# Attention stage of a sandwich layer: a loop over two halves written out, with the second half's taps interleaved with the first half's last products

## The chip, the cores and the metric

One core of one Trainium2 chip runs the whole program in one launch. The metric is device time in microseconds. Engines: PE is the matrix engine (with its weight loads, PEld, beside it), DVE the vector engine, ACT the scalar engine, POOL the GpSimd, and SP issues most transfers. Each engine runs its own instructions in program order; they meet at semaphores.

## What is computed

x is 4 x 2048 rows of 256 floats. The first layer makes, for each row and head, 31 softmaxed weights from the row itself and sums the 31 rows up to it with them; the second is a mixture of experts behind a router. Everything is float32.

```python
def _L0_attn_ref(x, w_lin):                       # H = 16 heads, K = 31 taps, P = 30, R = 16
    w = jnp.einsum('btc,fc->btf', x, w_lin).reshape(B, T, H, K)
    w = jax.nn.softmax(w.astype(jnp.float32), axis=-1).astype(x.dtype)
    ...
    kidx = s_idx - t_idx + P
    mask = (kidx >= 0) & (kidx < K)
    ...
    out = jnp.einsum('bhts,bhsr->bhtr', we, xh)
...
def _L0_ffn_ref(...):                             # 16 experts, top 2, and a shared expert
    shared = jax.nn.silu(x @ shared_w_gate.T) * (x @ shared_w_up.T) @ shared_w_down.T
    shared = shared * jax.nn.sigmoid(x @ shared_gate_w.T)
    logits = x @ gate_w.T
    ...
    out = expert_out + shared
x = x + _layernorm(_L0_attn_ref(_layernorm(x), w_lin))
x = x + _layernorm(_L0_ffn_ref(_layernorm(x), ...))
```

## The kernel before

The program has six parts in a row, each closed by a block: `attention`, `routing`, shared experts with the scatter, experts, and the shared-and-combine part. Only `attention` is touched. It computes both the first layer and, row by row, the normalised input `yn` of the second layer, its turned copy `ynt` and the router's logits.

`attention` works in two halves of 4096 rows (`HALVES`), in a hardware loop `Fori(0, HALVES)` on every engine. Each half has two stages.

**Taps stage**, 16 steps (`NPR`), each of two tiles of 128 rows (`u`). SP loads x (`load_x`), DVE takes mean and variance (`moments`), POOL makes scale and shift (`scales1`: add, subtract, power, multiply), ACT normalises (`normal`) into `xn`, SP stores it to a scratch tensor (`store_xn`). PE transposes it (`turn_x`), ACT and DVE split the result in a high and a low part (`high`, `low`), PE multiplies each tile with the weights in three products per half of the channels (`taps`: 12 matmuls of 512 columns a step), DVE takes the maximum and subtracts it (`spread`), ACT takes the exponential (`exps`), PE transposes it (`turn_e`, 8 transposes) and ACT copies it to `probs` (`keep`). The weights `wraw` are loaded once, split by ACT into `wh` (line 415) and by DVE into `wl` (line 328).

**Products stage**, 16 steps (`NCH`), each of two tiles (`t`). SP loads x's normalised rows back in four transfers (`load_xs`, into `xbd`) and the residual x (`load_xr`). DVE spreads the probabilities over a band with a mask (`masked`, four operations), PE multiplies (`products`, 128 matmuls of 68 columns in two groups of 64, line 528), DVE divides by the sums and takes moments (`divided`), POOL makes scales (`scales23`), ACT normalises (`centred`), POOL adds the residual (`residual`), DVE takes the moments of the sum (`moments3`), ACT makes `yn` (`normal2`), PE transposes it (`turn_yn`, line 541), ACT copies it to `ynt` (`turned`, line 474), PE multiplies it with the router weights (`router`, line 548), ACT copies the result to `logits` (`put_logits`, line 453), SP stores x2, yn and ynt. This chain is spread over seven steps by the offsets given to `skewed`: with offset -5, `turn_yn` in step i works on tile pair i - 5. Within a step each engine's order is the order of the arguments. `skewed` writes the first and last steps of a stage out and puts the middle ones in a loop, four steps to a turn.

```python
skewed(pe, NCH, (-5, turn_yn), (0, lambda i, q: products(i, q, 0)), (-5, router),
       (0, lambda i, q: products(i, q, 1)))
skewed(act, NCH, (-6, put_logits), (-2, centred), (-4, normal2), (-5, turned))
skewed(ve, NCH, (1, masked), (-1, divided), (-2, moments3))
skewed(po, NCH, (-2, residual), (-1, scales23), (-3, nothing))
```

PSUM has eight banks `pb`. In the taps stage the transposed x has banks 0 and 1, the logits of the taps 2 to 5, the transposed exponentials 6 and 7; in the products stage the products have 0 to 3, and `psy` (the turned yn of tile t and beside it its router result) banks 6 and 7. Since each stage drains before the next begins, the banks can be given twice.

Ahead of the loop POOL sets all constants (among them zeros in `xbd`, line 262, and the masks, lines 273 to 281); SP and PE wait for all of them (`CONSTS`), and PE also for the whole of `wl` and for the router weights. ACT issues eight small transfers (line 418) that give the store semaphores their first value. Behind the loop DVE runs the search for the two best experts on the first 56 of 64 tiles (`top.find`, lines 118 to 124).

## Time and profile before

| | |
|---|---|
| median of three runs | 1187.29 us (1184.39 to 1193.31) |
| profiled execution | 1188.04 us, of which the profile's span is 1186.0 |
| busy over the span | PE 982.8 us (83%), DVE 808.8 (68%), ACT 581.0 (49%), POOL 482.3 (41%) |
| granted PE clock, mean | 0.92 |
| attention part | 0 to 436.7 us of the span |
| bytes moved | 188.07 MB, mean 159 GB/s |

How to read it: the busy shares are means over stages with different limits, so each stretch is read by itself. Times are from the span's start. An idle time in square brackets stands before the operation and names who ended it.

### The profile page before, as it was taken

What the parts mean: (1) busy time and instruction counts of PE and PEld (TensorE: products, weight loads), DVE (VectorE), ACT (ScalarE), POOL (GpSimd) and SP (SyncE); (2) the same over time, 40 slices, a digit from 0 to 9 for tenths busy, and PEclk for the clock granted to TensorE, in tenths of its full rate; (3) what the DMA queues carried; (4) which work ended last, traced back from release to release, by engine and by line L of the source; (5) the groups of instructions that cost most, each with busy time, mean ns of one, the idle gap of its engine ahead of it and who ended that gap; (6) DMA issues with size and microseconds to landing.
All of it is one profiled execution on the core that took longest, in us unless ns stands there. A gap on an engine that the chain in (4) does not pass through costs nothing. (4 is left out here: it accounts for less than half of the span.)

```text
span 1186.0 us, 31172 instructions
## 1 busy us (share of the span) xinstructions
PE 982.8 (83%) x9192; PEld 849.6 (72%) x9193; DVE 808.8 (68%) x2070; ACT 581.0 (49%) x1308; POOL 482.3 (41%) x725
## 2 busy tenths in 40 slices
PE   3998798499879840799999869998999799989981
PEld 2777686377678830688888768888888687878771
DVE  3887987188798779444445347777777468777765
ACT  3993344499534441344444435554555345444442
POOL 5221445222054533576676500000000357888774
PEclk9998999599999955899999989999999899989995
DMA  3333577443247762757565454555555435656553
GB/s 107 108 99 81 152 209 213 131 120 108 64 129 219 213 216 98 232 188 242 191 201 173 153 142 155 160 161 160 153 162 160 151 116 178 183 188 183 174 162 106
DMA packets 189971, 188.07 MB, mean 159 GB/s; under 512 B 56256, under 2 KB 171072, under 8 KB 189632
## 3 DMA queue, kind: packets, MB, share of 16 engines
q1 hardware_dynamic: 173232, 150.30, 42.2%
q0 software_dynamic: 12288, 33.57, 8.6%
q10 hardware_dynamic: 4368, 3.16, 0.9%
q8 instruction: 43, 0.70, 0.3%
q14 instruction: 40, 0.33, 0.1%
HBM read 100.81 MB, written 86.15 MB: 158 GB/s over the span
## 5 line engine op out<-in xcount | busy, mean ns | idle before, releaser
L903 POOL DMA_INDIRECT sorted_rows<-yr,sl x128 | 133.6, 1044 | 81.5 <-issue 38.0
L1192 POOL DMA_INDIRECT cy<-expert_rows,csl x128 | 138.8, 1085 | 45.4 <-issue 44.2
L528 PE MATMUL bank<-xbd,am 128*32 128x68 f32 x4096 | 138.5, 304 | 11.3 <-DVE am L367 4.4
L528 PEld LDWEIGHTS bank<-xbd,am 128*32 128x32 f32 x4096 | 122.8, 129 | 18.6 <-DVE am L367 10.9
L1185 POOL MEMSET czero<- 128x4 f32 x1 | 0.1, 102 | 257.8 <-POOLq L968 257.8
L1065 PE MATMUL bank<-eh,xh 128*128 x288 | 95.3, 331 | 0.7 <-DVE xl L1109 0.7
L367 DVE TENSOR_TENSOR am<-probs,mask 128x512 f32<-128x512 f32 x128 | 82.5, 707 | 18.8 <-PE bank L528 9.3
L805 DVE TENSOR_TENSOR s_hf<-s_sg,bank 128x512 f32<-128x512 f32 (+1 forms) x48 | 33.0, 688 | 88.3 <-ACT s_sg L780 88.3
L287 POOL TENSOR_TENSOR rstd<-mv,eps 128x2 f32<-128x2 f32 (+1 forms) x68 | 13.5, 198 | 187.3 <-DVE mv L359 110.9
L1109 DVE TENSOR_TENSOR xl<-bank,xh 128x256 fp32r<-128x256 f32 x144 | 61.2, 425 | 41.7 <-ACT xh L1091 40.7
L1091 ACT ACTIVATE xh<-bank 128x256 fp32r<-128x256 f32 x144 | 55.5, 385 | 67.8 <-PE bank L1038 67.6
L458 ACT ACTIVATE av<-av,shift,rstd 128x256 f32<-128x256 f32 x64 | 35.0, 595 | 105.6 <-POOL shift L292 105.6
L1038 PE MATMUL bank<-ident,xg 128*128 128x128 f32 x288 | 56.8, 280 | 33.6 <-issue 22.6
L1065 PE MATMUL bank<-el,xh 128*128 x288 | 82.3, 286 | 0.0
L1065 PE MATMUL bank<-eh,xl 128*128 x288 | 82.0, 285 | 0.0
L823 PE MATMUL bank<-c_yh,gh 128*128 128x512 f32 x176 | 73.4, 417 | 6.3 <-DVE c_yl L797 6.3
L302 POOL TENSOR_TENSOR x<-av,xr 128x256 f32<-128x256 f32 x64 | 47.4, 761 | 72.4 <-ACT yn L466 69.5
L823 PE MATMUL bank<-s_yh,gh 128*128 128x512 f32 x176 | 71.0, 403 | 6.1 <-DVE s_yl L797 6.1
L782 ACT ACTIVATE c_hh<-c_hf 128x512 fp32r<-128x512 f32 (+1 forms) x48 | 30.3, 632 | 91.3 <-DVE c_hf L805 91.3
L834 PE MATMUL bank<-dh,c_hh 128*128 128x256 f32 (+1 forms) x192 | 58.6, 305 | 19.0 <-DVE c_hl L810 19.0
L823 PE MATMUL bank<-c_yl,gh 128*128 128x512 f32 x176 | 72.0, 409 | 0.0
L823 PE MATMUL bank<-c_yh,gl 128*128 128x512 f32 x176 | 71.5, 406 | 0.0
(198 smaller groups left out, 3155.8 us busy)
## 6 DMA issues: line engine op xcount, KB each, us to landing
xg<-sorted_rows SPq DMA_DIRECT2D x144, 128.0 KB, 2.1
expert_rows<-yo SPq DMA_DIRECT2D x144, 128.0 KB, 1.8
xbd<-xn_scratch SPq DMA_DIRECT2D x128, 72.0 KB, 2.2
xt<-x SPq DMA_DIRECT2D x32, 256.0 KB, 2.7
xn_scratch<-xn SPq DMA_DIRECT2D x64, 128.0 KB, 2.5
xr<-x SPq DMA_DIRECT2D x32, 256.0 KB, 3.2
x_scratch<-x SPq DMA_DIRECT2D x32, 256.0 KB, 3.2
yn_scratch<-yn SPq DMA_DIRECT2D x32, 256.0 KB, 3.1
```

Source lines behind the costliest of these rows:

```text
L302: nc.gpsimd.tensor_tensor(x2[:, q, t], av[:, q, t], xr[:, q, t], ALU.add).then_inc(s["x2_ok"], 1)
L367: nc.vector.tensor_tensor(am[:, q, g], probs[:, bass.ds(i * CB, CB), g, None, :].to_broadcast([P, CB, 2, J]), mask[:, None].to_broadcast([ ...
L458: nc.scalar.activation(av[:, q, t], av[:, q, t], ACT.Identity, scale=rstd2[:, q, t:t + 1], bias=shift2[:, q, t:t + 1]).then_inc(s["z_ok"], 1)
L528: ins = nc.tensor.matmul(pso[q][t][J * b:J * b + J, g * MW:(g + 1) * MW], am[:, q, g, e, side], xbd[:, q, e + side, :, g], start=(g == 0 a ...
L823: ins = self.nc.tensor.matmul(self.pb[2 * k + half][:], w[:, c, col:col + P], y[:, q, c, :], start=(j == 0), stop=(j == 5))
L834: ins = self.nc.tensor.matmul(o, a[0:f, g, t * P:(t + 1) * P], w[0:f, m, :], start=(m == 0 and t % 2 == 0 and j == 0), stop=(m == FT - 1 a ...
L903: nc.gpsimd.indirect_dma_start(out=xg_d, out_offset=bass.IndirectOffsetOnAxis(ap=sl[:, q, t, u, k:k + 1], axis=0), in_=yr[:, t, u], in_off ...
L1038: ins = nc.tensor.transpose(px[r % 2][:, c * P:(c + 1) * P], xg[:, r, c * P:(c + 1) * P], ident[:])
L1065: ins = nc.tensor.matmul(pg[r % 2][:, 0:2 * MF], a[:, r % 2, c * P:(c + 1) * P], w[:, bass.ds(e, 1), c * C:(c + 1) * C], start=(j == 0), s ...
L1091: nc.scalar.activation(xh[:, r % 2], px[r % 2][:, 0:C], ACT.Copy).then_inc(s["xh_ok"], 1)
L1109: nc.vector.tensor_tensor(xl[:, r % 2], px[r % 2][:, 0:C], xh[:, r % 2].bitcast(F32), ALU.subtract).then_inc(s["xl_ok"], 1)
L1192: nc.gpsimd.indirect_dma_start(out=y[:, v, k, j], out_offset=None, in_=yg_d, in_offset=bass.IndirectOffsetOnAxis(ap=sl[:, v, k, j:j + 1], ...
```

## The change

The loop over halves and the loops inside it are gone; each engine's instructions are written out in one common order, `flow`. It goes through the taps steps of half 0, its product steps, and from product step 13 on sets a taps step of half 1 (beginning with -4, whose only work is a load of x) behind each product step, up to product step 22, which is past the last work of half 0. The remaining taps steps and the product steps of half 1 follow. To let both stages be in flight, the banks are shared out anew: both transposed tiles of x share bank 0, the transposed exponentials have banks 1 and 6, both `psy` tiles share bank 7, and tiles of one bank are waited for as a pair. The router's offset goes from -5 to -6, and it now stands at the head of PE's step, `turn_yn` between the two groups of products. The router's result overwrites the turned rows.

At the start the weights are loaded in two parts on ACT's queue, split in two parts, and PE waits for each where it first uses it; x's first load waits for no constants; POOL sets xbd, the masks and other constants in the first taps steps (`places`). The eight first stores are gone, and the padding rows of all four sequences are stored once.

```diff
-        psx, psl, pse = pb[0:2], (pb[2:4], pb[4:6]), pb[6:8]
-        pso, psy = (pb[0:2], pb[2:4]), pb[6:8]
+        psx, psl, pse = (pb[0][:, 0:C], pb[0][:, C:2 * C]), (pb[2:4], pb[4:6]), (pb[1], pb[6])
+        pso, psy = (pb[0:2], pb[2:4]), (pb[7][:, 0:C], pb[7][:, C:2 * C])
...
+        def flow(taps_step, product_step):
+            for i in range(-4, NPR):
+                taps_step(0, i)
+            for j in range(2):
+                taps_step(0, NPR + j)
+                product_step(0, j - 2)
+            for i in range(NCH - 3):
+                product_step(0, i)
+            for i in range(NCH - 3, NCH + 7):
+                product_step(0, i)
+                taps_step(1, i - NCH - 1)
+            for i in range(6, NPR):
+                taps_step(1, i)
+            for j in range(2):
+                taps_step(1, NPR + j)
+                product_step(1, j - 2)
+            for i in range(NCH + 7):
+                product_step(1, i)
+
+        def at(h, i, f):
+            if 0 <= i < 16:
+                f(h * 16 + i)
...
-            sp.dma_start(wraw[:], wd).then_inc(s["w_in"], 16)
-            sp.dma_start(gws[:], gw).then_inc(s["gw_in"], 16)
-            sp.wait_ge(s["consts"], CONSTS)
...
+            def load_xs(n):
+                q = n % 2
+                if n == 0:
+                    wait_apart(sp, s["sp_passed"], s["padded"], 64)
+                    wait_apart(sp, s["sp_passed"], s["places_ok"], PLACES)
+                if n % NCH == 0:
+                    for k in range(2):
+                        wait_apart(sp, s["sp_passed"], s[f"xn_out{k}"], (n // NCH + 1) * (NPR * 16))
+                sp.wait_ge(s["pso_full"], n + 1)
...
+            def taps_step(h, i):
+                at(h, i + 4, load_x)
+                at(h, i + 2, store_xn)
+                if h == 0 and i == 0:
+                    sp.dma_start(gws[:], gw).then_inc(s["gw_in"], 16)
+                    sp.wait_ge(s["zeros"], 1)
+                    for a in range(BATCH):
+                        sp.dma_start(xn_d[a, 0], zero[0:J, 0:C]).then_inc(s["padded"], 16)
+
+            def product_step(h, i):
+                at(h, i + 2, load_xs)
+                at(h, i, load_xr)
+                at(h, i - 2, store_x2)
+                at(h, i - 4, store_yn)
+                at(h, i - 5, store_ynt)
+            flow(taps_step, product_step)
...
-            nc.gpsimd.memset(xbd[:], 0.0).then_inc(s["consts"], 1)
...
+            def places(i):
+                if i == 0:
+                    nc.gpsimd.memset(xbd[:, 0], 0.0).then_inc(s["places_ok"], 1)
+                if i == 1:
+                    nc.gpsimd.memset(xbd[:, 1], 0.0).then_inc(s["places_ok"], 1)
+                if i == 2:
+                    nc.gpsimd.memset(ones[:], 1.0).then_inc(s["consts"], 1)
+                    nc.gpsimd.memset(mask[:], 1.0).then_inc(s["consts"], 1)
+                    nc.gpsimd.iota(top.iota[:], pattern=[[-1, E]], base=E, channel_multiplier=0).then_inc(s["consts"], 1)
+                    po.wait_ge(s["consts"], 6)
+                    po.wait_ge(s["places_ok"], 2)
+                if 3 <= i < 3 + HS:
+                    k = i - 3
+                    part = slice(32 * k, 32 * k + 32)
+                    po.wait_ge(s["norm_ok"], i + 4)
+                    nc.gpsimd.memset(xbd[part, :, :, SLOT_C + k:SLOT_C + k + 1, :], 1.0).then_inc(s["places_ok"], 1)
...
+            def low(n):
+                ve.wait_ge(s["xth_ok"], n * 2 + 2)
+                for u in range(2):
+                    nc.vector.tensor_tensor(xtl[:, n % 2, u], psx[u], xth[:, n % 2, u].bitcast(F32),
+                                            ALU.subtract).then_inc(s["xtl_ok"], 1)
...
+            def taps_step(h, i):
+                at(h, i - 1, spread)
+                at(h, i + 1, low)
+                at(h, i + 3, moments)
+                if h == 0 and i == -2:
+                    for c in range(CC):
+                        ve.wait_ge(s["w_hi"], c + 1)
+                        nc.vector.tensor_tensor(wl[:, c], wraw[:, c], wh[:, c].bitcast(F32), ALU.subtract).then_inc(s["w_lo"], 1)
+
+            def product_step(h, i):
+                at(h, i + 1, masked)
+                at(h, i - 1, divided)
+                at(h, i - 2, moments3)
+            flow(taps_step, product_step)
...
+            for c in range(CC):
+                act.dma_start(wraw[:, c], wd[:, c]).then_inc(s[f"w_in{c}"], 16)
...
-            nc.scalar.activation(wh[:], wraw[:], ACT.Copy).then_inc(s["w_hi"], 1)
-            act.wait_ge(s["zeros"], 1)
-            for k, name in enumerate("xn_out0 xn_out1 x2_out0 x2_out1 yn_out0 yn_out1 ynt_out0 ynt_out1".split()):
-                act.dma_start(first_d[k], zero[:, 0:4]).then_inc(s[name], 16)
...
+            def high(n):
+                for u in range(2):
+                    m = n * 2 + u
+                    act.wait_ge(s["psx_full"], n * 2 + 2)
+                    act.wait_ge(s["psl_full"], m + 1)
+                    nc.scalar.activation(xth[:, n % 2, u], psx[u], ACT.Copy).then_inc(s["xth_ok"], 1)
...
+            def put_logits(n):
+                for t in range(2):
+                    m = n * 2 + t
+                    act.wait_ge(s["psg_full"], n * 2 + 2)
+                    nc.scalar.activation(logits[:, m:m + 1, :], psy[t][:, None, 0:GW], ACT.Copy).then_inc(s["lg_ok"], 1)
...
+            def taps_step(h, i):
+                at(h, i - 2, keep)
+                at(h, i + 1, high)
+                at(h, i - 1, exps)
+                if h == 0 and i == -2:
+                    weights_high(0)
+                at(h, i + 2, normal)
+                if h == 0 and i == -2:
+                    weights_high(1)
+
+            def product_step(h, i):
+                at(h, i - 6, put_logits)
+                at(h, i - 2, centred)
+                at(h, i - 4, normal2)
+                at(h, i - 5, turned)
+            flow(taps_step, product_step)
...
-            pe.wait_ge(s["consts"], CONSTS)
-            pe.wait_ge(s["w_lo"], 1)
-            pe.wait_ge(s["gw_in"], 16)
...
-                skewed(pe, NPR, (-2, turn_e), (1, turn_x), (0, taps))
...
-                skewed(pe, NCH, (-5, turn_yn), (0, lambda i, q: products(i, q, 0)), (-5, router),
-                       (0, lambda i, q: products(i, q, 1)))
...
+            def turn_x(n):
+                if n == NPR:
+                    pe.wait_ge(s["av_ok"], (NCH - 1) * 2 + 4)
+                for u in range(2):
+                    m = n * 2 + u
+                    pe.wait_ge(s["xn_ok"], m + 5)
+                    pe.wait_ge(s["xtl_ok"], n * 2 + 2)
...
+            def turn_yn(n):
+                for t in range(2):
+                    m = n * 2 + t
+                    pe.wait_ge(s["yn_ok"], m + 5)
+                    pe.wait_ge(s["lg_ok"], n * 2 + 2)
...
+            def router(n):
+                if n == 0:
+                    pe.wait_ge(s["gw_in"], 16)
+                pe.wait_ge(s["ynt_ok"], n * 2 + 2)
+                for t in range(2):
+                    for c in range(CC):
+                        ins = nc.tensor.matmul(psy[t][:, 0:GW], ynt[:, n % 2, t, c], gws[:, c, :],
+                                               start=(c == 0), stop=(c == CC - 1))
+                    ins.then_inc(s["psg_full"], 1)
...
+            def taps_step(h, i):
+                at(h, i - 2, turn_e)
+                at(h, i + 1, turn_x)
+                at(h, i, taps)
+
+            def product_step(h, i):
+                at(h, i - 6, router)
+                at(h, i, lambda n: products(n, 0))
+                at(h, i - 5, turn_yn)
+                at(h, i, lambda n: products(n, 1))
+            flow(taps_step, product_step)
```

## Rows read from the trace of the kernel before

**Rows 1.** Busy time by windows: start:end, length, each engine's busy us, granted clock, DMA share, GB/s

```profile
137.02:202.36 65.34, 58.95 (x1405) 51.83 (x1402) 54.62 (x156) 30.04 (x81) 31.29 (x60) 1.00 0.70 204
202.36:235.98 33.62, 16.16 (x68) 12.01 (x69) 7.33 (x27) 14.63 (x39) 9.15 (x24) 0.54 0.45 147
...
350.84:416.05 65.21, 60.15 (x1405) 53.04 (x1402) 54.08 (x156) 31.28 (x83) 31.33 (x61) 0.97 0.72 210
416.05:436.70 20.65, 13.30 (x60) 10.38 (x60) 15.40 (x27) 9.81 (x30) 7.35 (x16) 0.60 0.50 170
22.20:95.20 73.00, 72.31 (x366) 55.77 (x365) 62.38 (x148) 68.47 (x116) 17.23 (x56) 1.00 0.39 108
```

**Rows 2.** Waits from 140 to 200 us: total us, times, longest

```profile
PE bank L548 <- ACT ynt L474: 6.4, 6, 1.7
...
ACT yn L466 <- DMA yn_scratch<-yn: 2.2, 2, 1.1
```

**Rows 3.** Timeline of product steps: start us, us, engine, line, operation, count, idle time before

```profile
101.21 8.53 PE L528 MATMUL bank<-xbd,am 128*32 128x68 f32 x256 [2.19 <-DVE am L367]
...
126.57 0.92 PE L541 MATMUL bank<-ident,yn 128*128 128x128 f32 x4 [1.03 <-ACT yn L466]
...
162.79 0.66 PE L541 MATMUL bank<-ident,yn 128*128 128x128 f32 x4
...
163.06 2.50 DVE L367 TENSOR_TENSOR am<-probs,mask 128x512 f32<-128x512 f32 x4 [0.73 <-PE bank L528]
...
163.38 2.19 PE L528 MATMUL bank<-xbd,am 128*32 128x68 f32 x64
164.17 1.08 ACT L466 ACTIVATE yn<-x,shift,rstd 128x256 f32<-128x256 f32 x2
165.16 0.63 ACT L474 ACTIVATE ynt<-bank 128x256 f32<-128x256 f32 x2
...
165.50 1.41 POOL L302 TENSOR_TENSOR x<-av,xr 128x256 f32<-128x256 f32 x2 [2.37 <-ACT yn L466]
...
165.58 1.07 PE L548 MATMUL bank<-gws,ynt 128*128 128x18 f32 x8
...
166.33 0.19 ACT L453 ACTIVATE logits<-bank 128x18 f32 x1 [0.54 <-PE bank L548]
...
167.91 0.75 DVE L399 BATCH_NORM_STATS2 st<-x 128x6 f32<-128x256 f32 x2
```

**Rows 4.** Timeline of the start

```profile
0.81 1.28 ACT L411 ACT_TABLE_LOAD   x1 [0.81 <-PEq L1352]
...
5.68 1.91 ACT L415 ACTIVATE wh<-wraw 128x2048 fp32r<-128x2048 f32 x1 [3.59 <-DMA wraw<-wd]
5.69 3.75 ACTq L418 DMA_DIRECT2D first_stores<-zero  x8
...
7.63 2.35 DVE L328 TENSOR_TENSOR wl<-wraw,wh 128x2048 fp32r<-128x2048 f32 x1 [7.63 <-ACT wh L415]
...
12.24 7.47 SPq L207 DMA_DIRECT2D xt<-x  x3
15.06 0.75 DVE L356 BATCH_NORM_STATS2 st<-xt 128x6 f32<-128x256 f32 x2 [5.09 <-DMA xt<-x]
...
22.25 0.78 PE L504 MATMUL bank<-wh,xth 128*128 128x512 f32 x1
```

**Rows 5.** Timeline of SP's queue between the halves

```profile
218.04 3.59 SPq L249 DMA_DIRECT2D ynt_scratch<-ynt  x2
...
225.32 8.14 SPq L207 DMA_DIRECT2D xt<-x  x3
```

**Rows 6.** Timeline behind the last product of the second half

```profile
425.02 1.09 DVE L118 TENSOR_REDUCE best<-logits 128x56 f32<-128x896 f32 x1
...
430.48 1.89 PE L548 MATMUL bank<-gws,ynt 128*128 128x18 f32 x8 [0.57 <-ACT ynt L474]
...
432.21 1.28 PE L541 MATMUL bank<-ident,yn 128*128 128x128 f32 x4
```

More of the change, by code:

```diff
@@ L43 @@
 EPS = 1e-5
-CONSTS = 8 + 4 * HS
 def wait_apart(eng, passed, sem, value):
@@ L75, in build_program @@
         top = TopTwo(nc, logits, sb, ctx.enter_context(nc.semaphore("top_step")))
-        attention(nc, x, wd, gw, first_d, xn_d, yn_d, ynt_d, x2_d, ident, ones, neg_half, eps, logits, top, pb)
+        attention(nc, x, wd, gw, xn_d, yn_d, ynt_d, x2_d, ident, ones, neg_half, eps, logits, top, pb)
         sems = {n: ctx.enter_context(nc.semaphore("sh_" + n)) for n in Shared.SEMS}
@@ L142, in skewed, with attention @@
         step(i, i % 2)
-def attention(nc, x, wd, gw, first_d, xn_d, yn_d, ynt_d, x2_d, ident, ones, neg_half, eps, logits, top, pb):
+def attention(nc, x, wd, gw, xn_d, yn_d, ynt_d, x2_d, ident, ones, neg_half, eps, logits, top, pb):
     x_blk = x.rearrange("(h u) (b j) c -> h (u b) j c", h=HALVES, j=J)
     x_nat = x.rearrange("a (n p) c -> (a n) p c", p=P)
+    NPR = J // 2
     with ExitStack() as ctx:
@@ L265, in _ @@
             po.wait_ge(s["zeros"], 1)
[L266 removed]
+            po.wait_ge(s["consts"], 3)
             nc.gpsimd.affine_select(out=ident[:], in_=ident[:], compare_op=ALU.not_equal, fill=1.0, base=0,
[L268 to L282 removed]
@@ new lines, in normal2, with turned @@
+            def normal2(n):
+                q = n % 2
+                act.wait_ge(s["norm2_ok"], n // NCH * (NCH + 2) + n % NCH + 3)
+                if n > 1:
+                    act.wait_ge(s[f"yn_out{q}"], n // 2 * 16)
+                for t in range(2):
+                    nc.scalar.activation(yn[:, q, t], x2[:, q, t], ACT.Identity, scale=rstd2[:, q, 2 + t:3 + t],
+                                         bias=shift2[:, q, 2 + t:3 + t]).then_inc(s["yn_ok"], 1)
+            def turned(n):
+                q = n % 2
+                if n > 1:
+                    act.wait_ge(s[f"ynt_out{q}"], n // 2 * 16)
+                for t in range(2):
+                    act.wait_ge(s["psy_full"], n * 2 + 2)
+                    nc.scalar.activation(ynt[:, q, t], psy[t].rearrange("p (c t) -> p c t", c=CC), ACT.Copy
+                                         ).then_inc(s["ynt_ok"], 1)
```

489 lines of the change are left out of this document (211 added, 278 removed).

## Prediction

> **What bounds the kernel now.** I cut the attention part by stage in the view of busy time by windows, read inside the stages in order of time, and took the view of waits to see who was late. The attention part is four stages one after the other, twice taps and then products, and it ends at 436.7 of 1186.0 us [rows 1]; nothing behind it is touched. In the taps stage PE is busy 72.3 of 73.0 us, ACT 68.5 and DVE 62.4 [rows 1]: 16 steps of 4.56 us, full, nothing to win there. In the product stage (steps 6 to 15 of the first half) PE is busy 58.95 of 65.34 us, so 5.9 us of work per step of 6.5; DVE has 54.6 us [rows 1]. What stops PE there is the router: it waits for ACT's copy of the turned rows, 6.4 us in 60 [rows 2]. DVE, nearly as full, then waits for PE (0.73 us before its masks) [rows 3]. Three stretches are badly filled. First, 22.2 us before the first taps matmul [rows 4]. Second, the 33.6 us between the last product of half 0 (202.4) and the first taps of half 1 (236.0): PE has 16 us of busy time at a granted clock of 0.54, half of which is short work stretched by the lower of its two levels, 1.2 GHz [rows 1, 5]. Third, 20.65 us from the last product of half 1 to the end [rows 1].
>
> **The change, part by part.**
>
> *Start.* Before, SP's first load of x waits for all constants and is issued at 12.24; the first taps matmul is at 22.25, 10.0 us later [rows 4]. After, it waits only for a credit that ACT gives after issuing two weight loads and loading its table: 0.81, two issues of 0.47 (3.75 for eight), table 1.28, so 3.0 [rows 4]. Plus the same 10.0: 13.0. Now the halves of the weight split lie in this chain: ACT's second half copy (1.91/2 = 0.95) stands ahead of its first copy of turned x, DVE's second (2.35/2 = 1.2) ahead of its first low part; they overlap in part, I take +1. First taps at 14.0, a gain of 8. Bounds: 9 if the split hides, 6 if the transfers collide. The Trainium skill ("DMA: Bandwidth & Descriptors", Issuing engines are not separate DMA queues) speaks against part of this: loads issued from another engine run on the same DMA engines, so moving the weights to ACT's queue saves only issue time and x now lands beside 1 MB of weights; by it alone the gain would be nearer the lower bound. Before, the two did not overlap, so no trace shows it. The constants (xbd's zeros, masks) go to POOL's taps steps, where POOL works 17 of 73 us [rows 1]; they are not needed before the first products.
>
> *Product steps.* Before, PE does turn_yn, products, router, products within a step, and the router needs what ACT makes at the end of that very step: centred, normal2 1.08, turned 0.63 [rows 3]. After: router of the tile six back, products, turn_yn, products. Router finds its rows made a step ago; turn_yn finds yn made a step ago and needs the logits copied while the first 2.2 us of products run. So PE's wait goes. What is late next: ACT now starts a step with the logits copies (0.19 each [rows 3]), which wait for the router at the head of PE's step. Counting from PE's step start: router 1.07, a quarter for the handover, copies 0.4, so centred starts at 1.7, and takes 1.1 (same shape as normal2's pair); normal2 ends at 3.9, POOL's residual gives its first half at 4.7. DVE reaches moments3 4.85 after it began its masks (163.06 to 167.91), so at 5.0 [rows 3]. It fits, with 0.3 us to spare. PE needs 5.9, DVE about 5.85; I take 6.05 per step. Steps 0 to 4 stay. Steps 5 to 15 of half 0 took 75.8 us (126.57 to 202.36 [rows 3, 1]); after, 11 x 6.05 = 66.6, and step 5 also loses its wait for yn (1.0, of which I count 0.7): a gain of 9.9. Half 1 has the same pattern (60.15 busy of 65.21 [rows 1]) and took about 0.7 us less: 9.1. Off for the moments of half 1 put into steps 14 and 15 (a third of DVE's 3.9 us per taps step, so about 1.2 us each, most of it covered because step 15 has no masks): 0.5. Sum 18.5. Bounds: 21 (PE never waits), and 8 if half of the slack comes back as waits.
>
> *Between the halves.* Before, 61.0 us go from the last product of half 0 to the end of taps step 5 of half 1 (33.6 + 6 x 4.56, the second taps stage having the first's pace). After, in PE's order, from the last product: step 16 is router, logits wait, turn_yn, turn_x; it ends when ACT, behind a router of 1.07, has done copies, centred, normal2 and turned (0.4, 1.1, 1.1, 0.6) and the two of its taps operations that this step has, half of its 4.3 us: 6.5. Step 17 waits for ACT again, then turn_yn and a taps step without its transposes of the exponentials, about 4.4 together: ends at 11.6. Steps 18 to 20 carry a full taps step (4.56) and the router chain: router 1.07, logits back 0.95, turn_yn 0.66, so 7.2 each: 33.3. Step 21 has no turn_yn, 5.6; step 22 is a plain taps step, 4.6: 43.5. The transfers moved there: SP's x loads stand behind the store of the turned rows in each mixed step, which waits for turned, some 5 us into the step; an x load takes 2.8 us (12.24 to DVE's first statistics at 15.06 [rows 4]) and DVE wants it only at the end of the next step, so nothing waits. Gain 61.0 - 43.5 = 17.5, say 18. Upper bound: the empty stretch hides all but ACT's work of the drain (14.6, less 3 for taps already in it [rows 1]), 21.6. Lower bound 10, if every mixed step costs a further microsecond or more. Part of this gain is the jump back: SP's last issue before it ends at 221.6, and the first x load comes at 225.3 [rows 5].
>
> *End.* The drain gets longer, since the router is a step later and both tiles share a bank and are waited for as a pair. Before, six steps in 20.65 us. After, with PE at its lower level as in the rows (router 1.89, turn_yn 1.28 [rows 6]): step 16 4.5; step 17 5.6 (it holds centred of the last tile); steps 18 to 20 each router 1.9, copies 0.6, turn_yn 1.3, turned 0.7 and four handovers of a quarter, 5.4; step 21 router, copies and the last store about 3: 29.3. Loss 8.5. The search for the top two that stands beside it starts 9.0 us after the last product (425.0), when the last moments are done, and lasts nearly to the end, 11.4 [rows 6, 1]; after, it starts 3.4 later, so even with a fast PE the end is 3 later. Bounds of the loss: 3 and 12.
>
> *Nothing for:* the banks' new shares (every new wait on a pair is met half a microsecond before its user is free in the taps stage; if not, PE, which is full there, loses up to 0.3 a step, 10 in all), and register work of the loops, which is on no path.
>
> Sum: 8 + 18.5 + 18 - 8.5 = 36. The profiled execution took 1188.04, a span of 1186.0 and 2.0 around it, and is 0.75 over the median of the three runs, 1187.29; 1188 - 36 = 1152, and the median moves it by less than one.
>
> **The rivals.**
>
> *The step stays slow.* The put_logits copies now tie ACT's chain to PE's step start with 0.3 us to spare; POOL and DVE slow each other (a mask group of 2.5 us against longer ones in early steps), and ACT already waits for the yn store now and then, 2.2 us in two waits [rows 2]. If steps stay at 6.8 us, 18.5 us are missing: 1170. Against: the yn store gets more time, because normal2 starts 1.5 us later within the step.
>
> *Mixed steps block each other.* Each engine still runs in one fixed order, so turn_x stands behind turn_yn, which stands behind a copy. At 9 us per mixed step the boundary gives 10: 1160.
>
> *Slower: fetching unrolled code.* All 32 product steps, some 280 PE instructions each, become straight code. It decides if fetching slows a product step past 7 us, that is below 40 instructions per us: 32 x 1.1 = 35 us eat the gain, and 1195 would follow at 7.3. Against it: the first two product steps are already straight code, and 256 matmuls with as many weight loads ran in 8.5 us, 60 per us [rows 3]. The Trainium skill ("Runtime: NRT & Kernel Launch", Instruction fetch mechanics) says that sequential fetch is hidden and taken branches stall; the row and the gap of SP at the jump agree.
>
> *No change.* The overlap and the product gain both fail, start and end cancel (8 - 8.5): 1187.
>
> **How the numbers follow.** Forecast (1140 to 1163) 0.66; step stays slow 0.15; mixed steps block, or both in part (1160 to 1175), 0.07; no change 0.06; slower 0.06. Range 1142 to 1172: it leaves out no change, slower, and the tails of the bounds. About 1% is what a measurement can tell (12 us). Faster by over 1% (under 1175.4): 0.87; within: 0.07; slower: 0.06.
>
> **What would show it.** First taps matmul near 14; product steps at 6.0 us with no PE wait for ynt; first taps of half 1 some 9 us after the last product of half 0, not 33.6; the granted clock there above 0.9 instead of 0.54; the end stretch about 29 us, with routers at 1.9 us. In all, attention ending near 401. I am wrong if product steps stay over 6.5 us with a new wait on ACT's centred or DVE's moments3, if PE in the mixed steps waits long for put_logits, or if PE's idle time is put down to issue in straight code.

## Result, and the profile after

The changed kernel takes 1145.95 us (median of 4 runs, 1144.87 to 1146.46). Beside it on the same chip the kernel before took 1189.62. The ratio is 0.9635, with an interval of 0.9593 to 0.9676. A second comparison, made later with the experiments, gave 1144.3 us against 1187.17, ratio 0.9641 (0.9625 to 0.9657). The profiled execution has a span of 1144.2 us against 1186.0, which is 41.8 us shorter.

The page of the changed kernel: its busy times, and its instruction fetches (packets, MB, share of the DMA engines):

```profile
span 1144.2 us, 28387 instructions
...
PE 969.2 (85%) x9192; PEld 844.1 (74%) x9193; DVE 800.4 (70%) x2071; ACT 574.1 (50%) x1309; POOL 490.3 (43%) x726
...
q8 instruction: 53, 0.87, 0.3%
```

The attention part divides at events that the timeline shows in both traces. In the table, "between" runs from the last product of half 0 to the first product of half 1, and so contains half 1's taps. "End" runs from the last product of half 1 to the first instruction of the routing part. The experiments further down are in it too, so that they can be compared line by line.

| us | start | taps 0 | products 0 | between | products 1 | end | routing at |
|---|---|---|---|---|---|---|---|
| before | 22.3 | 79.0 | 101.2 | 113.2 | 100.5 | 20.7 | 436.7 |
| changed | 15.3 | 79.7 | 89.2 | 94.1 | 89.8 | 25.2 | 393.3 |
| changed, again (a1_again) | 15.3 | 79.0 | 89.9 | 93.8 | 89.2 | 25.7 | 392.9 |
| e1_no_mix | 15.4 | 79.8 | 89.2 | 112.4 | 89.2 | 25.8 | 411.7 |
| e2_router_back | 15.5 | 79.7 | 102.0 | 102.2 | 103.3 | 23.2 | 426.0 |
| e3_start_waits | 21.5 | 79.1 | 90.1 | 94.4 | 89.2 | 25.4 | 399.7 |
| e4_old_router_late | 22.4 | 79.2 | 92.9 | 117.3 | 92.9 | 24.9 | 429.5 |
| e5_act_06 | 15.7 | 78.6 | 89.7 | 93.9 | 89.2 | 25.8 | 392.9 |
| e6_act_24 | 15.7 | 78.8 | 89.6 | 100.6 | 89.2 | 28.7 | 402.6 |
| e7_drain | 15.3 | 79.8 | 89.2 | 94.5 | 89.8 | 23.6 | 392.2 |
| e8_drain_search | 15.4 | 79.0 | 89.2 | 94.9 | 89.6 | 22.7 | 390.7 |
| e9_act_13_products | 15.5 | 79.8 | 89.8 | 94.3 | 89.8 | 25.3 | 394.5 |
| e10_act_27_products | 15.8 | 79.1 | 94.1 | 93.6 | 94.1 | 26.0 | 402.7 |

The two executions of the changed kernel differ by up to 0.7 us in a stage and by 0.4 us at routing. Over all the executions a stage that an edit does not touch varies a little more (the first taps stage from 78.6 to 79.8), so a difference of about 1 us in one stage says nothing. The gains of the change are 6.9 at the start, 11.9 and 10.6 in the product stages and 19.1 between; it loses 0.7 in the first taps and 4.5 at the end. Together that is the 43.4 us by which routing begins earlier. Everything behind routing takes 1.6 us longer, 750.9 against 749.3, which gives the 41.8; the second execution of the changed kernel takes 748.4 there, so this 1.6 is not an effect of the change.

Busy time by windows in the changed kernel (columns as in [rows 1]): some nine product steps, the short stretch from the last product to the first taps of half 1, mixed steps, and the end. They answer to the lines of [rows 1]:

```profile
130.00:180.00 50.00, 50.00 (x1208) 44.57 (x1204) 47.44 (x141) 24.80 (x70) 28.70 (x53) 1.00 0.81 234
184.20:193.10 8.90, 4.88 (x33) 4.49 (x33) 7.12 (x28) 6.62 (x18) 6.67 (x17) 0.84 0.76 253
200.00:220.00 20.00, 19.11 (x117) 16.25 (x116) 13.26 (x34) 18.46 (x42) 4.76 (x16) 1.00 0.51 163
368.10:393.30 25.20, 15.45 (x71) 13.09 (x68) 15.84 (x30) 10.81 (x35) 8.54 (x19) 0.56 0.47 158
```

PE is busy for all of 50.00 us in the product steps, where it had 58.95 of 65.34. The 33.6 us hole between the halves is 8.9 us wide, and the steps behind it are full. The waits from 130 to 180 us (total, times, longest) answer to [rows 2]. PE's matmuls have none on the turned rows; its weight loads have four, of 0.2 us at most, while the matmuls before them still run:

```profile
...
ACT logits L510 <- PE bank L629: 12.7, 9, 1.5
ACT av L516 <- POOL shift L328: 12.2, 8, 1.6
...
PEld bank L629 <- ACT ynt L534: 0.9, 4, 0.2
```

One product step in the timeline (columns as in [rows 3]):

```profile
140.47 1.10 ACT L516 ACTIVATE av<-av,shift,rstd 128x256 f32<-128x256 f32 x2 [1.59 <-POOL shift L328]
...
140.62 0.66 PE L620 MATMUL bank<-ident,yn 128*128 128x128 f32 x4
...
141.21 2.19 PE L607 MATMUL bank<-xbd,am 128*32 128x68 f32 x64
...
142.46 0.63 ACT L534 ACTIVATE ynt<-bank 128x256 f32<-128x256 f32 x2
...
143.33 1.07 PE L629 MATMUL bank<-gws,ynt 128*128 128x18 f32 x8
...
144.43 0.26 ACT L510 ACTIVATE logits<-bank 128x18 f32<-128x18 f32 x2 [1.34 <-PE bank L629]
...
146.44 0.33 PE L620 MATMUL bank<-ident,yn 128*128 128x128 f32 x1
```

From 140.62 to 146.44 is one step, 5.82 us. The turned rows are ready at 143.09, just before the router at 143.33. The logits copies end at 144.69, and the next transposes of yn need them only at 146.44. ACT's centred copies do not start behind the logits: they wait 1.59 us more for POOL's scales.

### The profile page after: what moved, and what is told of

It reads as the page before. It is cut to its first block and busy times, and to the rows that moved or that the text cites. A ratio compares the mean times of both kernels' runs of the same rounds, so it can differ in the third digit from the quotient of the medians.

```text
span 1144.2 us, 28387 instructions
## 1 busy us (share of the span) xinstructions
PE 969.2 (85%) x9192; PEld 844.1 (74%) x9193; DVE 800.4 (70%) x2071; ACT 574.1 (50%) x1309; POOL 490.3 (43%) x726
## 5 line engine op out<-in xcount | busy, mean ns | idle before, releaser
L994 POOL DMA_INDIRECT sorted_rows<-yr,sl x128 | 138.3, 1080 | 77.5 <-issue 38.0
L1200 DVE TENSOR_TENSOR xl<-bank,xh 128x256 fp32r<-128x256 f32 x144 | 61.2, 425 | 42.9 <-ACT xh L1182 41.9
L408 DVE TENSOR_TENSOR am<-probs,mask 128x512 f32<-128x512 f32 x128 | 80.0, 688 | 8.4 <-ACT probs L502 7.5
L925 PE MATMUL bank<-dh,c_hh 128*128 128x256 f32 (+1 forms) x192 | 57.7, 300 | 25.2 <-DVE c_hl L901 25.2
L914 PE MATMUL bank<-s_yl,gh 128*128 128x512 f32 x176 | 70.3, 399 | 0.0
L914 PE MATMUL bank<-s_yh,gl 128*128 128x512 f32 x176 | 70.3, 399 | 0.0
```

Of the source, the lines that this page charges most:

```text
L408: nc.vector.tensor_tensor(am[:, q, g], probs[:, bass.ds(i * CB, CB), g, None, :].to_broadcast([P, CB, 2, J]), mask[:, None].to_broadcast([ ...
L914: ins = self.nc.tensor.matmul(self.pb[2 * k + half][:], w[:, c, col:col + P], y[:, q, c, :], start=(j == 0), stop=(j == 5))
L925: ins = self.nc.tensor.matmul(o, a[0:f, g, t * P:(t + 1) * P], w[0:f, m, :], start=(m == 0 and t % 2 == 0 and j == 0), stop=(m == FT - 1 a ...
L994: nc.gpsimd.indirect_dma_start(out=xg_d, out_offset=bass.IndirectOffsetOnAxis(ap=sl[:, q, t, u, k:k + 1], axis=0), in_=yr[:, t, u], in_off ...
L1200: nc.vector.tensor_tensor(xl[:, r % 2], px[r % 2][:, 0:C], xh[:, r % 2].bitcast(F32), ALU.subtract).then_inc(s["xl_ok"], 1)
```

## The experiments

The first four ran on one chip, where the kernel before takes 1257.13 us. On it the traces show the same stage times in attention, and the extra time lies behind routing: 806.4 to 815.6 us there, against 748.1 to 751.5 in the traces of the other chips. So they are compared through the table. Where a ratio is given, it is against the kernel before on the same chip. The changed kernel itself was not run there. The times of these four runs are 4 to 10 us better against the kernel before than their routing rows say (e1 35.4 us in time, 25.0 at routing); that difference lies behind routing, where the executions on this chip alone vary by 9 us, and it is not counted for any edit.

### e1_no_mix: the halves one after the other

The product stage of half 0 is run to its end, and half 1's taps begin only then. Everything else is as changed.

```diff
-            for i in range(NCH - 3):
+            for i in range(NCH + 7):
                 product_step(0, i)
-            for i in range(NCH - 3, NCH + 7):
-                product_step(0, i)
-                taps_step(1, i - NCH - 1)
-            for i in range(6, NPR):
+            for i in range(-4, NPR):
                 taps_step(1, i)
```

> The changed kernel with the two halves one behind the other again (all 23 product steps of half 0, then the taps steps of half 1), everything else kept. Theory: the interleaving itself brings the boundary's gain. In the changed kernel 94.1 us lie between the last product of half 0 and the first of half 1; without it I expect the old 113.2, less the 3.7 us of the jump back, plus 4 us for the longer drain, 113.5: so 19 us slower than the changed kernel, about 1165. Rival: writing the loop out is what helps (no jump, no register work), and the interleaving brings 10 or less: 1156 or less. The product steps should stay at 5.8 us by both.

Measured: 1221.78 us, ratio 0.9718 (0.9675 to 0.9761). "Between" is 112.4 against 94.1, and no other stage moves by more than the 0.7 us. The window from the last product to the first taps, which is 33.6 us wide again:

```profile
184.40:218.00 33.60, 16.73 (x77) 13.55 (x77) 8.13 (x31) 14.23 (x40) 11.15 (x29) 0.58 0.46 149
```

Busy times and clock are near those of the kernel before in [rows 1] (16.16 and 0.54). So the interleaving by itself gives 18.3 us, all of it here. Nothing of the gain in the product steps comes from it. e1 also shows what the jump at the loop's end had cost: SP's queue, which had stood idle for 3.7 us in front of its first load of half 1 [rows 5], now goes on at once:

```profile
203.09 4.60 SPq L260 DMA_DIRECT2D ynt_scratch<-ynt  x2
207.73 7.46 SPq L223 DMA_DIRECT2D xt<-x  x3
```

"Between" is only 0.8 us shorter than in the kernel before all the same, since the drain in front of it is longer: SP's last store ends 23.3 us behind the last product, where it was 19.3.

### e2_router_back: the router at its old place in the changed kernel

```diff
-                at(h, i - 6, router)
-                at(h, i, lambda n: products(n, 0))
                 at(h, i - 5, turn_yn)
+                at(h, i, lambda n: products(n, 0))
+                at(h, i - 5, router)
                 at(h, i, lambda n: products(n, 1))
```

> The changed kernel with the router back in the step of its transposes and between the two groups of products (offset -5). Theory: the router's place alone takes PE's wait out of the product steps; back come 0.45 to 0.7 us per step, some 20 us over both halves, partly offset by a shorter drain (3 less), and 4 more in the mixed steps, where router would stand right behind the transposes: 1165 to 1168. Rival: the product steps are faster because they are straight code without register work, and the router's place does little: 1150 or less.

Measured: 1239.96 us, ratio 0.9865 (0.9831 to 0.9898). The product stages are 102.0 and 103.3, "between" is 8.1 longer, and the end is 2.0 shorter. Waits of e2 from 140 to 190 us:

```profile
PEld bank L629 <- ACT ynt L534: 7.0, 4, 2.1
DVE am L408 <- PE bank L607: 6.8, 6, 1.6
PE bank L629 <- ACT ynt L534: 5.9, 4, 1.8
```

The waits of [rows 2] are back, and DVE's masks wait for PE. The loss was larger than expected: steps alternate, those with a wait take 7.3 us and the others 6.3, so a step is 1.0 us longer on average and not 0.45 to 0.7. All of the gain in the product stages, 12.8 and 13.5 us, hangs on the place of this one call once the rest is changed. It is more than was gained: with the router back the stages are slower than in the kernel before (101.2 and 100.5). In e2 both tiles of a step share one bank and are waited for as a pair, where the kernel before has a bank for each; how much of the loss is due to that was not separated. It also earns 8.1 in the mixed steps, which the prediction had not credited to it.

### e4_old_router_late: only the router moved, in the kernel before

```diff
-                skewed(pe, NCH, (-5, turn_yn), (0, lambda i, q: products(i, q, 0)), (-5, router),
+                skewed(pe, NCH, (-6, router), (0, lambda i, q: products(i, q, 0)), (-5, turn_yn),
```

> The kernel before with one edit: PE's order is router of the tile pair six back, products, transposes, products. Loops, banks and everything else stay. Theory: this alone removes PE's wait in both product stages, 20 us, and costs 3 at each of the two drains: 14 us faster than before, ratio 0.988. Rival: the loops' register work or the banks hold the step, nothing is gained and the drains cost: 1.000 to 1.005.

Measured: 1244.1 us, ratio 0.9897 (0.9865 to 0.9928). The product stages gain 8.3 and 7.6, and the two drains lose 4.1 and 4.2, so routing begins 7.2 earlier. The expectation had 14. Both terms were off: 16 of gain instead of 20, and 8 of loss instead of 6. The median is 13.0 us below that of the kernel before, close to the 14, but only 7.2 of it lies in the part that was edited. In the PE timeline of e4 most steps take 5.9 us, and some still wait:

```profile
167.15 0.66 PE L541 MATMUL bank<-ident,yn 128*128 128x128 f32 x4
167.74 2.18 PE L528 MATMUL bank<-xbd,am 128*32 128x68 f32 x64
170.68 1.07 PE L548 MATMUL bank<-gws,ynt 128*128 128x18 f32 x8 [0.76 <-ACT ynt L474]
```

So the move alone brings 15.9 of the 22.6 us that the product stages gained. The changed kernel is 3.7 and 3.1 us per stage faster than this. Which of its other parts removes these last waits (straight code, the logits and the turned rows on one bank, ACT's order) was not separated.

### e3_start_waits: the constants ahead of the first load again

POOL makes all its constants first, and SP's loads wait for them. The weight split stays in halves.

```diff
+            wait_apart(sp, s["sp_passed"], s["places_ok"], PLACES)
...
-                if h == 0:
-                    places(i)
...
+            for i in range(3 + HS):
+                places(i)
+            po.wait_ge(s["places_ok"], PLACES)
```

> The changed kernel with POOL setting all constants first and the first load of x waiting for them, as before; the weights keep their two parts and their queue. Theory: the start's gain is the wait for the constants, and all of it reaches the end, since the taps stage is full: first taps at 22.3 instead of 15.3, 7 us slower, 1153. Rival: the early steps catch up, or the weights' load was the gain: 1149 or less.

Measured: 1215.74 us, ratio 0.9679 (0.9642 to 0.9716). First taps come at 21.5 instead of 15.3, and routing at 399.7 instead of 393.3. The 6.2 us of the wait reach the end of attention whole. The first load and its landing in e3, and the same in the changed kernel:

```profile
10.13 7.94 SPq L228 DMA_DIRECT2D xt<-x  x3
13.03 0.75 DVE L397 BATCH_NORM_STATS2 st<-xt 128x6 f32<-128x256 f32 x2 [13.03 <-DMA xt<-x]
```

```profile
3.04 8.84 SPq L226 DMA_DIRECT2D xt<-x  x3
4.72 1.06 ACT L473 ACTIVATE wh<-wraw 128x1024 fp32r<-128x1024 f32 x1 [1.70 <-DMA wraw<-wd]
6.85 0.75 DVE L395 BATCH_NORM_STATS2 st<-xt 128x6 f32<-128x256 f32 x2 [6.85 <-DMA xt<-x]
```

In e3, long after the weights, x takes 2.9 us from issue to use. Beside the weights it takes 3.8. So about 0.9 us of the start is the price of loading both at once.

### e5_act_06 and e6_act_24: more work on ACT in every step

Both add work that is no part of the reference: copies of a zero tile into a spare one, behind the logits copies of each step. There is one in e5 and four in e6 (the spare tile comes with them).

```diff
+                for k in range(1):
+                    nc.scalar.activation(spare[:, k], zero[:], ACT.Copy)
```

> The changed kernel with one more ACT operation of 0.6 us (a copy of 128x256 zeros into a spare tile) in each product step, behind the logits copies and ahead of centred. The prediction counted 0.3 us to spare at this place: by that, each of some 22 full product steps grows by 0.3, 7 us, about 1153. The rival reading, of the trace after: ACT stands idle 1.6 us behind the logits copies, until POOL's scales are there, so nothing is on the path: 1146 to 1148.

> The same with four such operations, 2.4 us, in each product step. With 1.6 us of idle time there, 0.8 us per step are not covered, 18 us over 22 steps, and some 5 to 10 in the drains: 1170 to 1175. By the prediction's count (0.3 to spare) 2.1 us per step are not covered: 46 us and the drains, 1195 or more.

Measured: e5 1145.29 us, ratio 0.9646 (0.9622 to 0.9669), no stage moved. Its one copy takes 0.42 us and not 0.6, so by the prediction's count it would have cost only 0.1 us a step, and e5 decides nothing between the two readings. e6 1152.6 us, ratio 0.9698 (0.9672 to 0.9723). The product stages do not move (89.6 and 89.2), "between" is 6.5 longer, and the end 3.5. The dose was mis-sized in this expectation too. In e6 the four copies take 1.33 us together and not 2.4:

```profile
193.79 1.33 ACT L513 ACTIVATE spare<-zero 128x256 f32<-128x256 f32 x4
```

So e6 says only that 1.3 us more on ACT are free in a product step. It doesn't say where the room ends, nor whether the 10 us it lost belong to the mixed steps and the end alone. The next two runs ask that.

### a1_again, e9_act_13_products, e10_act_27_products: the dose in product steps only

```diff
+                for k in range(8 if n % NCH < 9 else 0):
+                    nc.scalar.activation(spare[:, k], zero[:], ACT.Copy)
```

e9 has four in the place of eight. This work too is no part of the reference.

> The changed kernel once more, unedited, beside the next two on one chip, so that their stages and times are compared with it and not with an execution on another chip. Every theory: 1145 us, attention's last product of half 1 near 368 and the search's results near 393, product stages of 89 to 90 us.

> The edit adds work that is no part of the reference: four copies of a zero tile behind the logits copies, 1.34 us together in the run e6, but only for tiles 0 to 8 of each half, whose steps are pure product steps; the mixed steps and the drain are as in the changed kernel. Theory A, that PE sets the step and ACT has 1.6 us idle behind its centred copies: nothing moves, product stages 89 to 90, attention's end within 1 us of the changed kernel's, and then the 9.3 us that e6 lost all came from the mixed steps and the drain. Theory B, the prediction's, that the logits copies tie ACT's chain to PE's step start with 0.3 us to spare: each of 18 steps longer by about 1.0 us, 9 per stage, attention's end 18 later.

> The same edit with eight copies, some 2.7 us in each of the 18 steps (an estimate, twice the 1.34 of e6). Theory A: 2.7 less the idle 1.6 stays, 1.1 us per step, stages of about 99, attention's end 20 later, 1165. Theory B: 2.4 us per step, stages of about 111, the end 43 later, 1188. Theory C, that the chain through ACT has more room than its one idle spell, because every handover of the ring has a step's depth of buffers: stages within 2 us of the changed kernel's, and the time within 5 us of it.

Measured, on one chip: 1144.3 us (1143.01 to 1145.95) for the changed kernel, 1147.0 (1145.44 to 1148.32) for e9 and 1154.27 (1151.96 to 1155.92) for e10. In e9 the four copies take 1.34 us, PE is busy for all of 50.00 us from 130 to 180, and the stages are those of the changed kernel; routing begins 1.6 us later, of which 1.0 is already there when the first taps stage ends, before any of the added work. In e10 both product stages are longer, by 4.2 and 4.8, and nothing else by more than 0.5. One ring of e10, in ACT and PE:

```profile
132.12 1.07 PE L632 MATMUL bank<-gws,ynt 128*128 128x18 f32 x8 [0.48 <-ACT ynt L537]
...
133.22 0.26 ACT L511 ACTIVATE logits<-bank 128x18 f32<-128x18 f32 x2 [1.16 <-PE bank L632]
133.37 2.56 ACT L513 ACTIVATE spare<-zero 128x256 f32<-128x256 f32 x8
...
135.83 1.09 ACT L519 ACTIVATE av<-av,shift,rstd 128x256 f32<-128x256 f32 x2
...
136.82 1.08 ACT L528 ACTIVATE yn<-x,shift,rstd 128x256 f32<-128x256 f32 x2
...
137.80 0.63 ACT L537 ACTIVATE ynt<-bank 128x256 f32<-128x256 f32 x2
...
138.48 1.07 PE L632 MATMUL bank<-gws,ynt 128*128 128x18 f32 x8 [0.51 <-ACT ynt L537]
```

Router, logits copies, added copies, centred, normal2, turned, next router: in this ring each operation now starts as soon as the one before it is done, and PE waits for the turned rows in every step. It takes 6.36 us. Without the 2.56 of added copies it is 3.8, and PE's own step is 5.82. So ACT has about 2.0 us of room in a product step. The same read from the stages: (2.56 - 2.0) x 9 steps = 5.0 us per stage, against 4.2 and 4.8 measured. The prediction's 0.3 us is refuted, by e9 (1.0 us per step by its count, and no stage moved) and by e10 (2.4 per step, 43 in all). Reading the room off ACT's one idle spell, 1.6 us, was too tight by 0.4, so my 20 for e10 was twice the 9.8 measured.

e9 also places what e6 lost: the same dose costs 9.7 us when it is in the mixed steps and the end too, and at most 1.6 when it is not.

### e7_drain and e8_drain_search: a shorter end

e7 puts, behind the last product of half 1, turn_yn before the router on PE, puts ACT's logits copies last in a step, and gives the odd tile pairs of half 1 a bank of their own (pb[6]), so that a transpose no longer waits for the logits of the pair just before it.

```diff
+        def psy(n, t):
+            bank = pb[6] if n > NCH and n % 2 else pb[7]
+            return bank[:, t * C:(t + 1) * C]
...
+                if h == 1 and i >= NCH:
+                    at(h, i - 5, turn_yn)
+                    at(h, i - 6, router)
+                    return
```

e8 adds to that a search for the top two over the first 24 tiles' rows, put into DVE's taps steps 1 to 5 of half 1, which are mixed steps, so that only 32 columns are left for the end instead of 56.

> The changed kernel with the end's chain opened: in half 1 the turned rows of odd tile pairs go to bank 6, which is free there, so turn_yn need not wait for the logits copy of the pair before; behind the last product PE does turn_yn ahead of router, and ACT does centred, normal2 and turned ahead of the logits copies. Theory: the chain router, copy, turn_yn, turned (4.24 us per step) sets the end; opened it takes about 3.6 per step, the last logits come 20 to 21 us behind the last product instead of 24.8, and the search starts 2.8 us earlier, so the end stretch falls from 25.2 to 21.5: 3 to 4 us faster than the changed kernel, 1142.5. Rival: the search on DVE or the last stores hold the end too, and 1 us or less is gained.

> The same, and the search over the first 24 of 64 tiles is done by DVE in the mixed steps (two of its ten operations a step, about 1 us, where DVE is busy 13 of 20 us), so the search behind the last moments covers 32 tiles and takes about 6.5 us instead of 11.4. Theory: the search no longer stands at the end, only the logits chain does: up to 1.5 us faster than the one before, 1141. Rival: DVE is late in the mixed steps and the gain is lost there: 1142.5 or slower.

Measured, with e5 and e6 on one chip: e7 1142.04 us, ratio 0.9615 (0.9595 to 0.9636); e8 1143.83, ratio 0.9615 (0.9591 to 0.9639). The intervals overlap that of the changed kernel, so against the kernel before neither is shown to be faster than the changed kernel. On this chip all five times of e7 (1140.33 to 1143.19) lie below all four of e5 (1144.25 to 1146.14), which differs from the changed kernel by idle work alone; those of e8 (1139.73 to 1144.13) do too. The changed kernel itself was not run beside them. In the table the end is 1.6 and 2.5 us shorter. e7 was meant to gain 3.7. Its timeline shows that PE's chain still waits, now once per step, in two steps for 3.11 us:

```profile
378.82 1.09 PE L630 MATMUL bank<-ident,yn 128*128 128x128 f32 x4 [3.11 <-ACT logits L514]
...
380.51 1.09 DVE L117 TENSOR_REDUCE best<-logits 128x56 f32<-128x896 f32 x1
...
390.62 1.09 DVE L120 TENSOR_REDUCE which<-a_pick 128x56 f32<-128x896 f32 x1
...
392.22 1.28 ACT L743 ACT_TABLE_LOAD   x1 [1.59 <-PEq L148]
```

The logits copies now stand behind centred, normal2 and turned on ACT, and the transposes behind them. The last logits come 22.0 us behind the last product (24.8 in the changed kernel, 20 to 21 expected). The search was to start 2.8 us earlier and starts 11.9 us behind the last product, as in the changed kernel. What sets the end in e7 is DVE's search, from 380.51 to about 391.7, while the last logits are copied at 390.63. In e8 the search ends earlier, and the logits are last again.

## Why the prediction was right, and where its steps were not

The forecast was 1152, and 1146 was measured: the gain was 41.8 in the profiled execution, not 36. The likeliest case was the one that happened, and each of its four mechanisms is found in the runs. The terms:

| us | predicted | bounds | measured |
|---|---|---|---|
| start | 8 | 6 to 9 | 6.9 |
| product steps | 18.5 | 8 to 21 | 22.6 |
| between the halves | 18 | 10 to 21.6 | 19.1 |
| end | -8.5 | -12 to -3 | -4.5 |
| first taps stage | 0 | | -0.7 |
| behind routing | 0 | | -1.6 |

The errors of the terms are -1.1, +4.1, +1.1, +4.0, -0.7 and -1.6, which is the 5.8 between 36 and 41.8. The two large ones both made the forecast too cautious.

**Start.** First taps were to come at 14.0 and come at 15.3. The mechanism stands (e3: the wait was worth 6.2). What was short is above all the load: 3.8 us beside the weights and not 2.8, the lower bound's reason. The chain from there to the first taps takes 8.5 us against 7.2 before, where 1 had been allowed for the split. The Trainium skill ("DMA: Bandwidth & Descriptors", Issuing engines are not separate DMA queues) had said that loads issued by another engine share the same DMA engines; the trace agrees, at about 1 us.

**Product steps.** The mechanism is right and is shown by e2 and e4: the router's wait for ACT's last work of the step was the stall. Two steps of the working failed. The first is the size, 6.05 us per step. I had taken PE's 5.9 of work as the floor and added for DVE; the step is 5.82, and PE is never idle in it. Over the eleven steps of half 0 that is (6.05 - 5.82) x 11 = 2.5 us, and the measured 11.9 less the predicted 9.4 (9.9, less 0.5 for the moments put in) is 2.5. In half 1 it is 10.6 against 9.1, 1.5 more. The upper bound of 21, "PE never waits", was computed from the same 5.9, so it lay below what happened. The second is "it fits, with 0.3 us to spare". I had let ACT's centred start as soon as the logits copies are done. It starts 1.6 us after them, when POOL's scales come, and can be held up by 2.0 us without cost, as e10 shows. The chain that I feared was not the late one, and the rival that rested on it (0.15) deserved less.

**Between the halves.** The sum was 43.5 us from the last product to the end of taps step 5, and 41.1 were measured; its parts cancel, so that the 18 came as near to 19.1 as it did is in part luck: step 17 was 3.3 us longer than predicted, and steps 18 to 20 together 3.9 shorter. PE timeline of the changed kernel, which answers to [rows 5]:

```profile
184.13 1.07 PE L629 MATMUL bank<-gws,ynt 128*128 128x18 f32 x8
...
185.64 0.63 PE L620 MATMUL bank<-ident,yn 128*128 128x128 f32 x4 [0.44 <-ACT logits L510]
...
189.49 1.21 PE L629 MATMUL bank<-gws,ynt 128*128 128x18 f32 x8 [2.79 <-ACT ynt L534]
...
191.49 1.09 PE L620 MATMUL bank<-ident,yn 128*128 128x128 f32 x4 [0.79 <-ACT logits L510]
...
193.08 0.78 PE L584 MATMUL bank<-wh,xth 128*128 128x512 f32 x1
...
196.22 0.63 PE L584 MATMUL bank<-wl,xth 128*128 128x512 f32 x1
...
197.35 0.43 PE L584 MATMUL bank<-wl,xth 128*128 128x512 f32 x1
...
197.88 0.96 PE L629 MATMUL bank<-gws,ynt 128*128 128x18 f32 x8
```

First taps come 8.9 us after the last product, against 9 predicted. Step 16 is 5.4 us long, not 6.5. Step 17, which I had at 5.1, is 8.4 (189.49 to 197.88): PE had waited 2.79 us for the turned rows, and its next transposes took 1.09 us where they take 0.63, its taps matmuls 0.63 where they take 0.43 from 197.07 on. Steps 18 to 20 were to take 7.2 each, 21.6 in all, and take 17.7. There I had added a full 0.95 us for the way of the logits to ACT and back, of which PE waits 0.44; and step 18 has no transposes of the exponentials yet (they start at 205). The clock was expected above 0.9 there. It is 0.84 up to the first taps, 0.50 from 191 to 197, and 1.00 from 200 to 220.

**End.** Steps 16 and 17 came as sized (4.3 and 5.7 against 4.5 and 5.6). Steps 18 to 20 were to take 5.4 us and take 4.23. One of them in the changed kernel:

```profile
382.25 1.90 PE L629 MATMUL bank<-gws,ynt 128*128 128x18 f32 x8 [0.81 <-ACT ynt L534]
...
384.19 0.26 ACT L510 ACTIVATE logits<-bank 128x18 f32<-128x18 f32 x2 [1.99 <-PE bank L629]
...
384.59 1.09 PE L620 MATMUL bank<-ident,yn 128*128 128x128 f32 x4 [0.44 <-ACT logits L510]
...
385.78 0.66 ACT L534 ACTIVATE ynt<-bank 128x256 f32<-128x256 f32 x2 [0.35 <-PE bank L620]
...
386.49 1.78 PEld L629 LDWEIGHTS bank<-gws,ynt 128*128 128x128 f32 x8 [1.21 <-ACT ynt L534]
```

The chain is 1.90 + 0.26 + 1.09 + 0.66 = 3.91, and the four handovers add 0.04, 0.14, 0.10 and 0.05, 0.33 in all. I had charged a quarter of a microsecond for each, which no row showed, 0.6 for the copies and 1.3 for the transposes. The largest failed term is the handover, 1.0 charged and 0.33 measured; the copies (0.26) and the transposes (1.09) make 0.55 more. A handover can't be read off a row's printed idle time either, since that contains work of the other engine: the 0.44 before the transposes holds the 0.26 of the copies. The second half of the step was right: the search starts 11.9 us after the last product instead of 9.0, 2.9 later (predicted 3.4), and in e7, where PE's chain is shorter, the end is still 2.9 longer than before.

**The rivals.** Mixed steps that block (9 us each) did not come: steps 18 to 20 take 5.3 to 6.3. Only step 17, at 8.4, was near it. Fetching straight code did not slow anything: 1208 matmuls and 1204 weight loads ran in 50 us, 48 per us, with PE busy throughout, and the fetched instructions rose only from 0.70 to 0.87 MB. The Trainium skill ("Runtime: NRT & Kernel Launch", Instruction fetch mechanics) says that sequential fetch is hidden; the trace agrees. Where the prediction has taken branches stall, the Trainium skill says it of a branch whose target isn't in the two blocks of instructions at hand. That e1 has 0.04 us in front of SP's first load, where the jump had 3.7, agrees with it but does not show what the time went to.

**A second look at size.** e1 puts interleaving at 18.3 of the 43.4 us at routing, and e3 puts the start wait at 6.4. e2 puts the router's place at 32.7, not to be added to the others: it also decides how well mixed steps run, and it is the loss from taking the move out of the changed kernel, where the old place costs more than it did in the kernel before. Put into the kernel before, the same move gives 15.9 in the product stages and 7.2 at routing, and PE still waits for the turned rows twice from 140 to 190 us, 1.5 us in all.

## What to carry to other kernels

When a matrix engine waits in each step for a copy that its partner made last in the same step, issue the dependent product one step later and put it first. Here that one move is worth 26 us in the product stages of the changed kernel, but 16 in those of the kernel before, and 7 net there, since it does not remove every wait and makes both drains longer. The gap between two stages needed the next stage's steps laid beside the drain. To find how much room an engine has, don't read its idle spell; add known work in the place that matters until the step grows, and check what the added work really takes in the trace. Price a chain in a drain by the end of one row and the start of the next, not by the idle time printed beside it.

## What the hardware showed that was not expected

A wait of 2.79 us on PE, in a stretch where ACT, DVE and the DMA engines were busy (186.7 to 189.5 us), was followed by some 7 us at the lower level of 1.2 GHz though PE then had work: the granted clock was 1.00 up to 190 us, 0.64 from 190 to 191, 0.50 from there to 197, and 1.00 again from 198. So it fell when PE had already begun to work again. Interleaving removed the long gap, and this is what is left of it.

The chip of e1 to e4 differs from the others behind routing. There, POOL, which issues the indirect stores of the sorted rows, stood idle before them for 141.0 us (e3); in the second execution of the changed kernel, on another chip, for 77.7:

```profile
L996 POOL DMA_INDIRECT sorted_rows<-yr,sl x128 | 128.0, 1000 | 141.0 <-DVE sl L1035 79.8 <-issue 38.1 <-DMA yr<-yn_scratch 22.8
```

```profile
L994 POOL DMA_INDIRECT sorted_rows<-yr,sl x128 | 137.7, 1076 | 77.7 <-issue 38.0 <-DMA yr<-yn_scratch 22.7 <-DVE sl L1033 16.6
```

The first line is e3's group of instructions, the second a1_again's. The waits for DVE's slots, 79.8 against 16.6, account for the difference, and behind routing e3 takes 65.6 us longer than a1_again. The traces lead past DVE. In the same stretch of e3 ACT stands idle in front of `s_sg`, the activation of the shared experts, with no instruction of this core named as what ended the wait (total us, times, longest):

```profile
ACT s_sg L873 <- remote: 61.2, 11, 9.9
```

All four executions on this chip have such waits before `s_sg`, 61.2 to 72.6 us in 10 to 12 waits, and none of the other nine has one. DVE's `s_hf` needs what ACT makes there, and DVE's slots stand behind `s_hf` in its queue. That this is the whole of the difference is not shown, and what ACT was held by stays open.
